# Another place for the feed-forward steps of the last two batches, and the last addition and store in two halves

## The chip, the cores and the metric

The kernel runs on one core of one Trainium2 chip. The metric is the device time of one execution in microseconds; 862.51 us is the median of three runs of the kernel before.

## What is computed

The reference is one decoder layer on x of 8 batches x 128 rows x 512 columns, float32: a latent attention with 128 heads, a cross attention with 32 query heads and 8 key heads, and a feed-forward with a router. Each is added to x after a layer norm. Only the third part is touched by the change:

```python
gate_logits = jnp.einsum('bsd,ed->bse', x, gate_w)
weights, selected = jax.lax.top_k(gate_logits, K)            # E = 8, K = 2
weights = jax.nn.softmax(weights.astype(jnp.float32), axis=2).astype(x.dtype)
result = jnp.einsum('bsd,od->bso', x, base_w) + base_b
w_full = jnp.sum(jax.nn.one_hot(selected, E, dtype=x.dtype) * weights[..., None], axis=2)
low = jnp.einsum('bsd,erd->ebsr', x, lora_A)                 # R = 16
lora_out = jnp.einsum('ebsr,eor,bse->bso', low, lora_B, w_full)
result = result + SCALING * lora_out
```

and the layer's output is `x + result`, where the x under the feed-forward is the normed one.

## The kernel before

The first 640 us are the latent attention, in 32 groups of four heads. Cross attention and feed-forward follow in one pipeline over all 8 batches, from about 640 us to the end. Every engine runs its own written-out list, a Python loop over u from FIRST = -8 to LAST - 1 = 40. A u below 32 is a unit of eight query heads, four units to a batch. With b, r = (u+1)//4, (u+1)%4 each step also does a piece of the batches on either side: r chooses the piece, b the batch. The order on an engine is the order of the code in this loop; engines wait for each other by semaphores, and each runs its list strictly in turn.

The steps after the last cross attention unit are the ones at issue. Batches are counted from 0 here, so the seventh is batch 6 and the eighth batch 7. For one batch v the feed-forward goes through these stages:

- x2 (L1104, VectorE): the cross attention's product is added to xs.
- norm_stats(2, v) (L1008 to L1010, VectorE) takes mean and variance; inverse(2, v) (L547, GpSimd) takes the power -0.5; norm_rows(2, v) (L1017, VectorE) writes the normed rows pn. GpSimd then adds the bias to xs (L555, semaphore s_xb).
- norm_turn(2, v) (L1432, TensorE) transposes pn into PSUM bank bF[0]; norm_high (L709, ScalarE) copies it as float16, Ah; norm_low (L1023, VectorE) keeps the remainder, Al.
- The gate product (L1156 through parts, 12 matmuls of 136 columns, agh and agl) writes the router's logits and the low-rank values into bank bF[1] = 7; ScalarE copies them to low (L753).
- gate_first (L1053 to L1061, VectorE) ranks the 8 logits, ScalarE takes the exponential (L745), gate_last (L1066 to L1071) makes the two weights and multiplies low by them.
- TensorE transposes low (L1444), ScalarE copies it as lowT (L742), and the low-rank product (L1462, float32) is added to the base product (base, L1156 with bwh and bwl, 12 matmuls of 512 columns) that waits in its own PSUM bank.
- x3 (L1088, VectorE) adds that bank to xs, and SyncE stores the batch (L434, result).

base_bank puts the base product of batches 0 to 5 into bank 7, that of batches 6 and 7 into banks 2 and 3. Bank 7 is also that of the gate product and of the cross attention's output product. Before each of these writes the helper take makes TensorE wait for whoever read the bank last:

```python
if r == 2:
    if 0 <= b - 2 < B:
        v = b - 2
        pe.wait_ge(n_tl[2], v + 1)
        take(bF[1], s_ge, v + 1)
```

So the gate product of batch 6 (u = 33) waits for x3 of batch 5, which reads bank 7 at u = 32. Behind that gate product, in the same step of TensorE's list, stand the four transposes of the last attention rows (L1477), which lead to O2h (L759), O2l (L1093) and the output product of batch 7. x_outputs (L1041 and L1045, VectorE) divides one unit's attention output by its sums and writes it to O2.

The last steps have these numbers: u = 32 is r = 1 with x3 of batch 5, norm_low and norm_turn of batch 6; u = 33 is r = 2; u = 34 is r = 3 with x2 of batch 7; u = 35 is r = 0 with norm_rows of batch 7; u = 36 is r = 1 with x3 and the low-rank product of batch 6 and the turn of batch 7; u = 37 is the gate product of batch 7; u = 40 has the low-rank product and x3 of batch 7.

Of the kernel before, what the change touches and what calls it, by code (L numbers as in the profile page):

```python
# [9 lines left out]
ALU = mybir.AluOpType  # L10
# [45 lines left out]
def build(nc, x, ctxT, pos, wdkr, wup, wqr, wo, xwq, xwkv, xwo, bw, ag, lb, bb, out):  # L56
    es = ExitStack()
    with es:
# [207 lines left out]
        def base_bank(v):  # L266

            return bF[1] if v < B - 2 else 2 + v % 2
# [48 lines left out]
        def _(sp):  # L317
# [114 lines left out]
            def result(b):  # L432
                sp.wait_ge(s_x3, b + 1)
                sp.dma_start(out[b], xs[:, b, :]).then_inc(s_out, 16)  # L434
# [7 lines left out]
            sp.wait_ge(s_out, 16 * B)  # L442
# [145 lines left out]
        def _(act):  # L588
# [145 lines left out]
            for u in range(FIRST, LAST):  # L734
                b, r = (u + 1) // KT, (u + 1) % KT
                turned_out(u)
                if r == 1 and 0 <= b - 3 < B:
                    v = b - 3
                    act.wait_ge(s_lt, v + 1)
                    if v >= 2:  # L740
                        act.wait_ge(s_f, v - 1)
                    nc.scalar.activation(lowT[:, v % 2], PS[:, 0, 3 * S:], ACT.Copy, scale=WS).then_inc(s_lT, 1)  # L742
# [3 lines left out]
                if r == 1:  # L746
                    norm_high(2, b - 2, bF[0], s_f)
# [25 lines left out]
        def _(dve):  # L773
# [275 lines left out]

            def gate_first(b):  # L1050
# [29 lines left out]
            for u in range(FIRST, LAST):  # L1080
                b, r = (u + 1) // KT, (u + 1) % KT
                if r == 1:
                    norm_low(2, b - 2, bF[0])
                    if 0 <= b - 3 < B:
                        v = b - 3
                        dve.wait_ge(s_f, v + 1)
                        dve.wait_ge(s_xb, v + 1)
                        nc.vector.scalar_tensor_tensor(xs[:, v, :], PS[:, base_bank(v), :], 1 / WS, xs[:, v, :],  # L1088
                                                       ALU.mult, ALU.add).then_inc(s_x3, 1)
# [17 lines left out]
                if 0 <= u - 1 < NU:  # L1107
                    x_outputs(u - 1)
                if r == 0:
                    norm_rows(2, b - 2)  # L1110
                    if 0 <= b + 1 < B:
# [13 lines left out]
                if r == 3:  # L1125
                    if b - 1 == B - 1:
                        norm_stats(2, b - 1)
                    if 0 <= b - 2 < B:
                        gate_last(b - 2)
                    if b - 1 < B - 1:  # L1130
                        norm_stats(2, b - 1)
# [18 lines left out]
        def _(pe):  # L1150
# [284 lines left out]
            for u in range(FIRST, LAST):  # L1435
                b, r = (u + 1) // KT, (u + 1) % KT
                if u == -2:
                    pe.wait_ge(s_x1, B)
                if r == 1 and 0 <= b - 3 < B:
# [15 lines left out]
                if r == 1:  # L1455
# [7 lines left out]
                    norm_turn(2, b - 2, bF[0])  # L1463
# [73 lines left out]
```

## Time and profile before

| what | value |
|---|---|
| median of three runs | 862.51 us (861.93 to 864.9) |
| the profiled execution, its own time | 860.44 us |
| its span in the profile | 858.5 us |
| mean granted TensorE clock | 0.98 |
| busy share of TensorE, VectorE, ScalarE, GpSimd | 93%, 75%, 66%, 68% |

A time in the profile is counted from the span's start. The span is that of the instructions; the execution's own time is 1.9 us longer. Rows give start, duration, engine, line and operation; in brackets stands how long the engine sat idle before it and for whom. PE is TensorE, PEld its weight load, DVE VectorE, ACT ScalarE, POOL GpSimd, SPq the queue of SyncE.

### The profile page before, as it was taken

To read this page: it belongs to the slowest core of one execution; us is meant where nothing else is said; L and a number is where in the kernel's file an instruction comes from. 1 tells how busy PE (TensorE), PEld (TensorE's weight loads), DVE (VectorE), ACT (ScalarE), POOL (GpSimd) and SP (SyncE) were. 2 spreads that over 40 slices of the span, in tenths; PEclk is the share of its full clock that TensorE was granted. 3 is DMA by queue.
4 is the path that set the end of the run, shared out by engine and by line. 5 is a ranking of instruction groups with operands and counts; after the bars stand their busy time and mean duration, and the time that the engine had idled before them with its cause. 6 is when DMAs were issued, how large, how long until landed. Compare 5 with 4: busy or idle time off the path is not lost.

```text
span 858.5 us, 17869 instructions
## 1 busy us (share of the span) xinstructions
PE 796.8 (93%) x5624; PEld 393.2 (46%) x5624; DVE 641.3 (75%) x1209; ACT 568.0 (66%) x1045; POOL 583.0 (68%) x493
## 2 busy tenths in 40 slices
PE   4999999999999999999999999999838688999986
PEld 3464444445444444444454444444313344555442
DVE  7867676767677888767888767788687567888754
ACT  4757777777777778777777777777530455555541
POOL 7747888888788888888788878885443323333210
PEclk9999999999999999999999999999978789999999
DMA  9345355434334343445323443432130000000001
GB/s 337 111 166 147 87 161 173 133 93 107 109 90 106 83 111 79 101 102 125 90 78 95 107 109 93 109 90 59 29 89 0 1 2 2 15 13 15 13 13 38
DMA packets 51227, 74.69 MB, mean 87 GB/s; under 512 B 9968, under 2 KB 33520, under 8 KB 50672
## 3 DMA queue, kind: packets, MB, share of 16 engines
q1 hardware_dynamic: 51184, 74.18, 31.7%
q8 instruction: 20, 0.33, 0.2%
q14 instruction: 23, 0.19, 0.1%
HBM read 38.16 MB, written 18.87 MB: 66 GB/s over the span
## 4 chain that ended last, share of the span: by engine, by line
PE 83%; DVE 9%; ACT 2%; issue 2%; SPq 1%; DMA 1%; POOL 0%; DVEq 0%; ACTq 0%
PE PS L1204 39%; PE PS L1156 8%; PE PS L1240 7%; PE PS L1272 6%; PE PS L1274 6%; PE PS L1289 5%; PE PS L1417 2%; PE PS L1424 1%; PE PS L1250 1%; PE PS L1386 1%; PE PS L1403 1%; PE PS L1432 1%; PE PS L1331 1%; PE PS L1462 1%; DVE xm L1031 1%
## 5 line engine op out<-in xcount | busy, mean ns | idle before, releaser
L496 POOL TENSOR_TENSOR Pl<-PR,Ph 128x512 f16<-128x512 f32 x254 | 285.8, 1157 | 24.4 <-ACT Ph L672 24.4
L665 ACT ACTIVATE PR<-PS 128x512 f32<-128x512 f32 x256 | 152.7, 597 | 130.8 <-PE PS L1274 124.4
L799 DVE TENSOR_REDUCE mneg<-PS 128x4 f16<-128x512 f32 x256 | 172.1, 685 | 36.8 <-PE PS L1240 34.6
L1204 PE MATMUL PS<-XTh,Wh 128*128 128x512 f16 x512 | 194.6, 380 | 0.0
L1204 PE MATMUL PS<-XTh,Wl 128*128 128x512 f16 x512 | 193.7, 378 | 0.0
L1204 PE MATMUL PS<-XTl,Wh 128*128 128x512 f16 x512 | 193.4, 378 | 0.0
L787 DVE SCALAR_TENSOR_TENSOR QS<-PS,QC 64x512 f16<-64x512 f32 x256 | 175.4, 685 | 19.7 <-ACT QC L597 15.7
L597 ACT ACTIVATE QC<-PS 64x512 f16<-64x512 f32 x256 | 150.9, 589 | 10.6 <-PE PS L1204 4.3
L672 ACT ACTIVATE Ph<-PR 128x512 f16<-128x512 f32 x256 | 139.3, 617 | 0.0
L1240 PEld LDWEIGHTS PS<-KC,QC 112*128 112x128 f16 x1024 | 78.8, 97 | 62.0 <-issue 2.5
L478 POOL TENSOR_TENSOR Wh<-Wraw,wscale 128x1024 f16<-128x1024 f32 x32 | 60.6, 1893 | 67.1 <-PE PS L1204 63.9
L1240 PE MATMUL PS<-KC,QC 112*128 112x128 f16 x1024 | 99.3, 219 | 0.0
L1272 PE MATMUL PS<-QC,KC 113*128 113x512 f16 x256 | 97.7, 382 | 0.0
L1274 PE MATMUL PS<-QS,KS 128*128 128x512 f16 x256 | 97.2, 379 | 0.0
L1204 PEld LDWEIGHTS PS<-XTh,Wh 128*128 128x128 f16 x512 | 49.9, 97 | 65.0 <-issue 25.9
L547 POOL TENSOR_TENSOR rstd<-rstd,power 128x1 f32<-128x1 f32 x16 | 8.8, 550 | 103.2 <-DVE rstd L1010 103.2
L1204 PEld LDWEIGHTS PS<-XTh,Wl 128*128 128x128 f16 x512 | 49.4, 97 | 61.2
L892 DVE TENSOR_SCALAR mT<-PS 16x128 f16<-16x128 f16 x64 | 13.6, 212 | 79.3 <-PE PS L1250 79.3
L484 POOL TENSOR_TENSOR Wl<-Wraw,Wh 128x1024 f16<-128x1024 f32 x32 | 68.2, 2132 | 2.5
L1204 PEld LDWEIGHTS PS<-XTl,Wh 128*128 128x128 f16 x512 | 49.7, 97 | 38.9
L482 POOL TENSOR_TENSOR Wraw<-Wraw,wscale 128x1024 f32<-128x1024 f32 x32 | 60.6, 1895 | 0.2
L1331 PE MATMUL PS<-wo_sb,U 128*128 128x512 f32 x64 | 34.9, 680 | 13.0 <-DVE U L966 11.6
(214 smaller groups left out, 1165.6 us busy)
## 6 DMA issues: line engine op xcount, KB each, us to landing
Wraw<-in_wqr SPq DMA_DIRECT2D x32, 512.0 KB, 5.1
QS<-QC SPq DMA_DIRECT2D x64, 256.0 KB, 3.2
head_outputs<-OS SPq DMA_DIRECT2D x256, 40.0 KB
q_content_parts<-stg SPq DMA_DIRECT2D x12, 256.0 KB, 2.9
k_content_parts<-stg SPq DMA_DIRECT2D x12, 256.0 KB, 3.1
QC<-q_content_parts SPq DMA_DIRECT2D x128, 24.0 KB
KC<-k_content_parts SPq DMA_DIRECT2D x32, 96.0 KB
xs<-in_x SPq DMA_DIRECT2D x8, 256.0 KB, 4.3
```

What stands on the lines that cost most here:

```text
L484: nc.gpsimd.tensor_tensor(Wl[:, par], Wraw[:, par], Wh[:, par], ALU.subtract).then_inc(s_ws, 1)
L496: nc.gpsimd.tensor_tensor(Pl[:, b], PR[:, b % 4], Ph[:, b], ALU.subtract).then_inc(s_pl, 1)
L597: nc.scalar.activation(QC[0:RD, par, t, 2 * p + h, :], PS[RD * h:RD * (h + 1), bQ[c % 2], :], ACT.Copy, scale=1 / WS).then_inc(s_qh, 1)
L665: nc.scalar.activation(PR[:, b % 4, :], PS[:, bB[b % 2], :], ACT.Exp, scale=ATT_SCALE).then_inc(s_e, 1)
L672: nc.scalar.activation(Ph[:, b, :], PR[:, b % 4, :], ACT.Copy).then_inc(s_ph, 1)
L787: nc.vector.scalar_tensor_tensor(QS[0:RD, par, t, j, :], PS[RD * h:RD * (h + 1), bQ[c % 2], :], 1 / WS, QC[0:RD, par, t, j, :], ALU.mult, ...
L799: nc.vector.tensor_reduce(mneg[:, par, b // 4, :, b % 4], PS[:, bA[b % 2], :].rearrange("p (j k) -> p j k", j=GH), AX.X, ALU.max, negate=T ...
L1156: last = mm(PS[:, bank, 0:c1 - c0], xt[:, k], wt[:, k, c0:c1], start=(start and k == 0 and n == 0), stop=(stop and k == KT - 1 and n == 2))
L1204: last = mm(PS[:, bQ[c % 2], :], wt[:, par, k, p * P:(p + 1) * P], xt[:, k, sl], start=(k == 0 and n == 0), stop=(k == KT - 1 and n == 2))
L1240: last = mm(PS[:, bA[b % 2], j * S:(j + 1) * S], QC[0:MROW, par, b // 4, j, b % 4 * S:(b % 4 + 1) * S], KC[0:MROW, par, b * S:(b + 1) * S] ...
L1272: mm(PS[:, bB[b % 2], :].rearrange("p (j q) -> p j q", j=GH), KC[0:MROW + 1, par, b * S:(b + 1) * S], QC[0:MROW + 1, par, t, :, b % 4 * S: ...
L1274: mm(PS[:, bB[b % 2], :].rearrange("p (j q) -> p j q", j=GH), KS[:, b * S:(b + 1) * S], QS[:, par, t, :, b % 4 * S:(b % 4 + 1) * S], start ...
```

## The change

Line numbers in the headings of the hunks are those of the files.

- VectorE, u = 32: x3 of batch 5 stands behind x_outputs of unit 31 and no longer ahead of it.
- VectorE, u = 35: gate_last of batch 6 stands behind norm_rows of batch 7 (it was ahead of it, in u = 34).
- TensorE, u = 36: norm_turn of batch 7 stands ahead of the transpose of low and the low-rank product of batch 6; ScalarE's norm_high of batch 7 stands ahead of its copy of lowT.
- x3 of batch 7 becomes two additions of 256 columns, and its store two transfers of 128 rows x 256 columns; the last wait counts 9 stores.
- In x3 the wait for the bias (s_xb) stands ahead of that for the low-rank product (s_f), for all batches.

```diff
@@ -430,8 +430,10 @@
                     sp.dma_start(KQ[row:row + 1, u % 4, 0:UQ, :], xmT[REP * h:REP * (h + 1), u % 2, :]).then_inc(s_xmd[u % 2], 16)
 
             def result(b):
-                sp.wait_ge(s_x3, b + 1)
-                sp.dma_start(out[b], xs[:, b, :]).then_inc(s_out, 16)
+                for i in range(2 if b == B - 1 else 1):
+                    c = slice(i * DM // 2, (i + 1) * DM // 2) if b == B - 1 else slice(0, DM)
+                    sp.wait_ge(s_x3, b + 1 + i)
+                    sp.dma_start(out[b][:, c], xs[:, b, c]).then_inc(s_out, 16)
 
             for u in range(NU):
                 x_maxima(u)
@@ -439,7 +441,7 @@
                     result(u // KT - 3)
             for b in range(B - 3, B):
                 result(b)
-            sp.wait_ge(s_out, 16 * B)
+            sp.wait_ge(s_out, 16 * (B + 1))
 
         @block.gpsimd
         def _(pool):
@@ -734,6 +736,8 @@
             for u in range(FIRST, LAST):
                 b, r = (u + 1) // KT, (u + 1) % KT
                 turned_out(u)
+                if r == 1 and b - 2 == B - 1:
+                    norm_high(2, b - 2, bF[0], s_f)
                 if r == 1 and 0 <= b - 3 < B:
                     v = b - 3
                     act.wait_ge(s_lt, v + 1)
@@ -743,7 +747,7 @@
                 if r == 3 and 0 <= b - 2 < B:
                     act.wait_ge(s_gx, b - 1)
                     nc.scalar.activation(ex[:], ex[:], ACT.Exp).then_inc(s_gy, 1)
-                if r == 1:
+                if r == 1 and b - 2 != B - 1:
                     norm_high(2, b - 2, bF[0], s_f)
                 if r == 2 and 0 <= b - 2 < B:
                     v = b - 2
@@ -1047,6 +1051,14 @@
                 last.then_inc(s_xon, 1)
                 dve.wait_ge(s_xon, u + 1)
 
+            def x3(v):
+                dve.wait_ge(s_xb, v + 1)
+                dve.wait_ge(s_f, v + 1)
+                for i in range(2 if v == B - 1 else 1):
+                    c = slice(i * DM // 2, (i + 1) * DM // 2) if v == B - 1 else slice(0, DM)
+                    nc.vector.scalar_tensor_tensor(xs[:, v, c], PS[:, base_bank(v), c], 1 / WS, xs[:, v, c], ALU.mult, ALU.add
+                                                   ).then_inc(s_x3, 1)
+
             def gate_first(b):
                 dve.wait_ge(s_ge, b + 1)
                 lg = low[:, b % 2, E * R:AG]
@@ -1081,12 +1093,8 @@
                 b, r = (u + 1) // KT, (u + 1) % KT
                 if r == 1:
                     norm_low(2, b - 2, bF[0])
-                    if 0 <= b - 3 < B:
-                        v = b - 3
-                        dve.wait_ge(s_f, v + 1)
-                        dve.wait_ge(s_xb, v + 1)
-                        nc.vector.scalar_tensor_tensor(xs[:, v, :], PS[:, base_bank(v), :], 1 / WS, xs[:, v, :],
-                                                       ALU.mult, ALU.add).then_inc(s_x3, 1)
+                    if 0 <= b - 3 < B and b - 3 != B - 3:
+                        x3(b - 3)
                 if r == 2 and 0 <= b - 1 < B:
                     v = b - 1
                     dve.wait_ge(s_oT, v + 1)
@@ -1106,8 +1114,12 @@
                         dve.wait_ge(s_x2, v + 1)
                 if 0 <= u - 1 < NU:
                     x_outputs(u - 1)
+                if r == 1 and b - 3 == B - 3:
+                    x3(b - 3)
                 if r == 0:
                     norm_rows(2, b - 2)
+                    if b - 2 == B - 1:
+                        gate_last(B - 2)
                     if 0 <= b + 1 < B:
                         v = b + 1
                         dve.wait_ge(s_xq, v + 1)
@@ -1125,7 +1137,7 @@
                 if r == 3:
                     if b - 1 == B - 1:
                         norm_stats(2, b - 1)
-                    if 0 <= b - 2 < B:
+                    if 0 <= b - 2 < B and b - 2 != B - 2:
                         gate_last(b - 2)
                     if b - 1 < B - 1:
                         norm_stats(2, b - 1)
@@ -1436,6 +1448,8 @@
                 b, r = (u + 1) // KT, (u + 1) % KT
                 if u == -2:
                     pe.wait_ge(s_x1, B)
+                if r == 1 and b - 2 == B - 1:
+                    norm_turn(2, b - 2, bF[0])
                 if r == 1 and 0 <= b - 3 < B:
                     v = b - 3
                     pe.wait_ge(s_lw, v + 1)
@@ -1460,7 +1474,8 @@
                             base(v)
                         pe.wait_ge(s_lT, v + 1)
                         mm(PS[:, base_bank(v), :], lowT[:, v % 2], lb_sb[:], start=False, stop=True).then_inc(s_f, 1)
-                    norm_turn(2, b - 2, bF[0])
+                    if b - 2 != B - 1:
+                        norm_turn(2, b - 2, bF[0])
                 if r == 2:
                     if 0 <= b - 2 < B:
                         v = b - 2
```

VectorE's list from Al of batch 6 (u = 32) to O2l of batch 7 (u = 33), before:

```order
L1023 TENSOR_TENSOR Al<-PS,Ah 128x512 [waits normed_high2]
L1088 SCALAR_TENSOR_TENSOR xs<-PS,xs 128x512 [waits bias_added,ffn_ready]
L1041 RECIPROCAL rz<-PS 128x2x2x2 [waits xo_turned]
L1045 TENSOR_TENSOR O_135<-PS,rz 128x2x32 [waits dve_chain]
L1045 TENSOR_TENSOR O_135<-PS,rz 128x2x32
L1093 TENSOR_TENSOR O2l<-PS,O2h 128x512 [waits oT_high,xo_out]
```

and in the changed kernel:

```order
L1027 TENSOR_TENSOR Al<-PS,Ah 128x512 [waits normed_high2]
L1045 RECIPROCAL rz<-PS 128x2x2x2 [waits xo_turned]
L1049 TENSOR_TENSOR O_135<-PS,rz 128x2x32 [waits dve_chain]
L1049 TENSOR_TENSOR O_135<-PS,rz 128x2x32
L1059 SCALAR_TENSOR_TENSOR xs<-PS,xs 128x512 [waits ffn_ready,bias_added,xo_out]
L1101 TENSOR_TENSOR O2l<-PS,O2h 128x512 [waits oT_high]
```

The addition of batch 5 moved past the three instructions of x_outputs.

VectorE's list from the variance of batch 7 (u = 34) to x3 of batch 6 (u = 36), before:

```order
L1010 TENSOR_SCALAR rstd<-mv 128x1 [waits dve_chain]
L1066 SCALAR_TENSOR_TENSOR ex<-rank,ex 128x8 [waits gate_exp]
L1067 TENSOR_REDUCE mx<-ex 128x1 [waits dve_chain]
L1068 RECIPROCAL mx<-mx 128x1 [waits dve_chain]
L1069 TENSOR_SCALAR ex<-ex,mx 128x8 [waits dve_chain]
L1071 TENSOR_TENSOR low<-low,ex 128x128 [waits dve_chain]
L1017 TENSOR_SCALAR pn<-xs,mv,rstd 128x512 [waits normed_turned2,rstd_ready2,low_weighted]
L1023 TENSOR_TENSOR Al<-PS,Ah 128x512 [waits normed_high2]
L1088 SCALAR_TENSOR_TENSOR xs<-PS,xs 128x512 [waits bias_added,ffn_ready]
```

and in the changed kernel:

```order
L1014 TENSOR_SCALAR rstd<-mv 128x1 [waits dve_chain]
L1021 TENSOR_SCALAR pn<-xs,mv,rstd 128x512 [waits normed_turned2,rstd_ready2]
L1078 SCALAR_TENSOR_TENSOR ex<-rank,ex 128x8 [waits gate_exp]
L1079 TENSOR_REDUCE mx<-ex 128x1 [waits dve_chain]
L1080 RECIPROCAL mx<-mx 128x1 [waits dve_chain]
L1081 TENSOR_SCALAR ex<-ex,mx 128x8 [waits dve_chain]
L1083 TENSOR_TENSOR low<-low,ex 128x128 [waits dve_chain]
L1027 TENSOR_TENSOR Al<-PS,Ah 128x512 [waits normed_high2,low_weighted]
L1059 SCALAR_TENSOR_TENSOR xs<-PS,xs 128x512 [waits ffn_ready,bias_added]
```

The normed rows of batch 7 moved ahead of the five instructions of gate_last of batch 6.

TensorE's list at u = 36, from the last matmul of the base product of batch 6 to the first of the gate product of batch 7, before:

```order
L1156 MATMUL PS<-bwh,Al 128x512
L1444 MATMUL PS<-ident,low 128x128 [waits xmax_out,kq_out,low_weighted]
L1462 MATMUL PS<-lb_sb,lowT 128x512 [waits lowT_out]
L1432 MATMUL PS<-ident,pn 128x128 [waits oT_low,normed2]
L1432 MATMUL PS<-ident,pn 128x128 x3
L1156 MATMUL PS<-agh,Ah 128x136 [waits x2_ready,normed_low2]
```

and in the changed kernel:

```order
L1168 MATMUL PS<-bwh,Al 128x512
L1444 MATMUL PS<-ident,pn 128x128 [waits oT_low,normed2]
L1444 MATMUL PS<-ident,pn 128x128 x3
L1458 MATMUL PS<-ident,low 128x128 [waits xmax_out,kq_out,low_weighted]
L1476 MATMUL PS<-lb_sb,lowT 128x512 [waits lowT_out]
L1168 MATMUL PS<-agh,Ah 128x136 [waits x2_ready,normed_low2]
```

The four transposes of pn moved ahead of the two steps on low and lowT; the gate product stands behind both in either list.

## Rows read from the trace of the kernel before

**Rows 1.** The page's part 4, the chain that ended last by engine.
```profile
PE 83%; DVE 9%; ACT 2%; issue 2%; SPq 1%; DMA 1%; POOL 0%; DVEq 0%; ACTq 0%
```
**Rows 2.** The chain in order of time, 835 to 843 us: start us, us, what.
```profile
836.10 0.69 DVE xs L1088
...
836.93 0.87 PE PS L1156 x12
...
838.27 0.61 ACT O2h L759
...
838.93 0.40 issue
839.33 0.70 DVE O2l L1093
```
**Rows 3.** Timeline of TensorE and VectorE, 827 to 837 us.
```profile
827.84 0.44 PE L1424 MATMUL PS<-ident,OW 128*128 128x128 f32 x2 [0.50 <-ACT OW L769]
...
828.39 0.21 DVE L1041 RECIPROCAL rz<-PS 128x8 f32<-128x8 f32 x1 [1.29 <-PE PS L1424]
...
835.90 0.44 PE L1424 MATMUL PS<-ident,OW 128*128 128x128 f32 x2 [0.50 <-ACT OW L769]
...
836.70 0.20 DVE L1041 RECIPROCAL rz<-PS 128x8 f32<-128x8 f32 x1
836.93 0.35 DVE L1045 TENSOR_TENSOR O<-PS,rz 128x64 f32<-128x64 f32 x2
```
**Rows 4.** The chain in order of time, 844 to 856 us.
```profile
845.53 0.30 DVE low L1071
...
846.58 1.13 PE PS L1462 x2
...
848.78 0.02 issue
848.81 0.70 DVE Al L1023
...
849.56 0.90 PE PS L1156 x12
850.48 0.29 ACT low L753
...
855.41 0.69 DVE xs L1088
```
**Rows 5.** Timeline of VectorE, TensorE and GpSimd around the third layer norm's steps.
```profile
844.85 0.55 POOL L547 TENSOR_TENSOR rstd<-rstd,power 128x1 f32<-128x1 f32 x1 [10.93 <-DVE rstd L1010]
...
847.54 0.60 PE L1432 MATMUL PS<-ident,pn 128*128 128x128 f32 x4
...
753.62 0.55 DVE L1017 TENSOR_SCALAR pn<-xs,mv,rstd 128x512 f32<-128x512 f32 x1
...
754.68 0.41 DVE L794 TENSOR_TENSOR rt<-PS,sinq 128x256 f32<-128x256 f32 x1
755.01 0.41 DVE L795 TENSOR_TENSOR rt<-PS,sinq 128x256 f32<-128x256 f32 x1
```
**Rows 6.** DMA: the stores (L434), the last one's packets, two small transfers' packets (822 to 826 us).
```profile
L434 SPq DMA_DIRECT2D y<-xs x8: 332/438/439, 747.7 to 856.1; - x8
DMA to landing us min/median/max: 2.0/2.1/2.4
q1 hardware_dynamic: 144, 0.26, 27.8%
q1 hardware_dynamic: 16, 0.00, 0.3%
```
**Rows 7.** Instruction transfers: the page, the window of 838.5 to 839 us, VectorE's stop at 688 us.
```profile
q8 instruction: 20, 0.33, 0.2%
q8 instruction: 1, 0.02, 11.6%
690.81 1.29 DVE L1031 TENSOR_REDUCE xm<-PS 128x4 f16<-128x512 f32 x2 [2.51 <-issue]
```

## The prediction

> **What bounds the kernel now.** The page's chain by engine [rows 1] is the first view: 83% of the path that sets the end runs through TensorE. The change leaves everything before 836 us as it is, so of that path only the last 22 us count. There, beside small waits, no work of a second kind runs: the chain in order of time goes from one engine to the next, and whatever makes one of its links later or earlier moves the end by as much. I read it in two pieces, 835 to 843 us [rows 2] and 844 us to the end [rows 4], and looked into the timelines for what stands beside it [rows 3, 5]. The store at the end needs the DMA views [rows 6], and one gap of VectorE the instruction transfers [rows 7].
>
> In the first piece [rows 2] the reader is to see that x3 of batch 5 is itself a link: VectorE adds it at 836.10 for 0.69 us, and the gate product of batch 6, which has to wait for bank 7, starts at 836.93, 0.14 us behind its end. The transposes of the last attention rows stand behind that gate product on TensorE, and on them hang O2h, O2l and the output product of batch 7. In the second piece [rows 4] the low-rank product of batch 6 and then the turn of batch 7 come one after the other on TensorE, and from the gate product of batch 7 at 849.56 on there is one line of steps to the last addition at 855.41.
>
> **Part A, x3 of batch 5 behind x_outputs.** This costs. x_outputs waits for the transposes at 835.90, which end at 836.34; at 827.84 to 828.28 the same pair was followed by VectorE 0.11 us later [rows 3], so it can start at 836.45, 0.25 us before its start of 836.70. The last of its three instructions ends 837.28 - 836.70 = 0.58 us later, at 837.03 [rows 3]. x3 follows after some 0.03 us of semaphore (what Al of batch 7 took behind its copy, 848.78 to 848.81 [rows 4]) and takes 0.69: it ends at 837.75, and the gate product starts 0.14 us later, at 837.89 in place of 836.93: 0.96 us late. The output rows that were given the earlier place are ready at 837.03 instead of 837.28, but TensorE reaches their transposes only behind the gate product, so that gain has no taker.
>
> Not all of the 0.96 arrives. O2h ends at 838.88, yet O2l starts at 839.33, with 0.40 us marked as issue [rows 2] where Al needed 0.03 us. Near it lies a transfer of instructions in 838.5 to 839 us, and a stop of 2.51 us with nothing to wait for is seen at 688 us too [rows 7]. I read both as VectorE waiting for its next code. If that stop runs from about 837 us to 839.33, a later O2h hides it: O2h ends at 838.88 + 0.96 = 839.84, O2l starts at 839.87, 0.54 us later than before. The ends are +0.54 and +0.96 (the stop remains as long as it is); nothing in the rows makes a gain possible while the gate product waits for bank 7. I take **+0.54**, since a stop that begins before the wait is nearest to what the 688 us row shows.
>
> **Part B, rows and turn of batch 7 ahead of gate_last and low-rank product of batch 6.** Before, GpSimd's power is done at 844.85 + 0.55 = 845.40, but pn stands behind gate_last, which runs until low's end at 845.53 + 0.30 = 845.83 [rows 4, 5]. Now pn can start at 845.43 and, at 0.55 us [rows 5], end at 845.98. gate_last is about 1.1 us long (from the variance just ahead of the power's start to 845.83), so low is weighted at 847.1 in place of 845.83. TensorE turns pn at 846.02, for 0.60 us [rows 5]; a copy to float16 takes ScalarE 0.61 (O2h [rows 2], of the same shape), to 847.27, and the remainder Al takes VectorE about 0.70 (O2l [rows 2], same shape), to 848.0. The low-rank product used to start 846.58 - 845.83 = 0.75 us behind low [rows 4], with a transpose and a copy between; now it starts at 847.85. ScalarE is free of Ah at 847.27 and so doesn't hold it. TensorE's next work started 847.54 - 846.58 = 0.96 us after the product's start [rows 4, 5]. So the gate product of batch 7 starts at 848.81, while its Al has been ready since 848.0: what is late next is the low-rank product of batch 6, not the rows. The gain is 849.56 - 848.81 = **-0.75**. Its ends: -0.58 if the product holds the next matmul for its whole 1.13 us [rows 4], and -0.9 if low's path is 0.15 shorter than worked out.
>
> x3 of batch 6 on VectorE starts when that product ends, near 849.0, and is done at 849.7; gate_first of batch 7 needs low at 848.81 + 0.92 + 0.29 = 850.02, where 0.92 is 850.48 - 849.56 [rows 4]. So it stays covered by 0.3 us. The base product of batch 7 runs beside the gate's chain in both kernels and shifts with it. The 5.9 us from the gate product to the last addition (855.41 - 849.56) keep their order.
>
> **Part C, last addition and store by halves.** An addition of 256 columns takes 0.41 us and the next one starts 0.33 us behind it [rows 5] (two on PSUM of that shape). The first half is done 0.41 us and both are done 0.74 us after the start, in place of 0.69 [rows 4]. SyncE issues a store in 0.44 us [rows 6], so the second can be issued 0.41 + 0.44 = 0.85 us after the start, 0.16 later than the whole one was. What it has for that is less to move: the last whole store takes 144 packets and 27.8% of 16 engines over 2.5 us, 11.1 us of engine time, or 85 ns for each of its 128 large packets of 2 KB, and 16 tiny packets take 0.3% of 4 us x 16, 12 ns each [rows 6]. A packet of 1 KB lies between; an estimate in the middle is 48 ns, and 8 per engine save 0.29 us. Net **-0.13**; the ends are +0.40 (1 KB costs 85 ns, the second half queues behind the first) and -0.42 (12 ns).
>
> The Trainium skill, DMA: Bandwidth & Descriptors, section Anatomy of one DMA, gives some 2.0 us of fixed cost and bytes over 436 GB/s, and its rules ask to coalesce small transfers. By it the half saves 0.30 us of moving, for which the second issue pays 0.16, so the sum would be the same within 0.01. [...]
>
> **Part D, the order of two waits.** In x3 the bias was added long before the product ends, at each of the two places that count, so the product's wait covers it in either order: 0.
>
> **Sum.** +0.54 - 0.75 - 0.13 = -0.34 us. The profiled execution took 860.44 us, so the changed kernel's would be 860.10. The median of three is 2.07 us above the profiled one, so on its scale I expect 862.2. No change in the clock is counted: all this lies within about 22 us, with engines idle no longer at a stretch than now.
>
> **Rivals.**
> *The code boundary lands on x3 of batch 5 (slower).* VectorE's stop belongs to a place in its instruction list. Between Al and O2l the list keeps the same instructions, but O2l's neighbours change, and the waits are packed otherwise. If the first instruction on the new code is now x3 and no longer O2l, VectorE stops ahead of an addition that TensorE waits for. The stop lasted 839.33 - 837.28 = 2.05 us at O2l and 2.51 at 688 us [rows 2, 3, 7]. From 837.03 on, x3 starts between 839.08 and 839.54, the gate product at 839.91 to 840.37, 3.0 to 3.4 us late; the old stop of 0.42 at O2l is gone, so A is +2.6 to +3.0, and the sum +1.7 to +2.1: 864.2 to 864.6, say 864.4. For it: the boundary lies within two or three instructions of x3. Against: the instruction count ahead of O2l is nearly the same, and then the stop falls where it did. It decides from one instruction's shift on. Chance 0.15. The Trainium skill, Advanced Engine Details and Errata, section ISA Cache, has lines of 16 KB or 256 instructions and two lines in all. The page's 20 transfers with 0.33 MB, 16.5 KB each [rows 7], agree with it.
>
> *Nothing is hidden.* The stop at O2l stays (A +0.96) and a packet of 1 KB costs as much as one of 2 KB (C +0.40): +0.96 - 0.75 + 0.40 = +0.61, 863.1. The tiny packets' 12 ns in [rows 6] speaks against the second half of it. Chance 0.15.
>
> *A isn't paid.* If the gate product of batch 6 did not have to wait for x3, or the earlier rows helped someone, the sum would be B and C alone: -0.88, 861.6. The 0.14 us between x3 and the gate product [rows 2] speak against it. Chance 0.1.
>
> **How the numbers follow.** The forecast has a chance of 0.6, at 862.2. A measurement of this kernel tells about 0.3% from no change, 2.6 us; forecast, second and third rival lie within it by far, and the first by 0.5 us or more unless C and B come at their bad ends. That gives slower 0.06, faster 0.03 (nothing in 22 us of chain offers 2.6 us but a stop that goes elsewhere), same 0.91. The three runs of before lie from 0.6 below to 2.4 above their median, so the range takes the rivals' 861.6 and 864.4 and some of that: 860.8 to 864.6.
>
> **What would show it.** Right: the gate product of batch 6 starts near 837.9 behind x3; O2l near 839.9 with no issue gap ahead of it; pn of batch 7 before gate_last; low-rank product of batch 6 directly ahead of the gate product of batch 7, which starts near 849.56 + 0.54 - 0.75 = 849.35; two additions of some 0.41 us at the end, and a second store with a shorter landing. Wrong: a gap of 2 us on VectorE ahead of x3 of batch 5 (first rival), one left ahead of O2l (second), the gate product of batch 6 still near 836.9 (third), or Al of batch 7 as the last thing its gate product waits for.

## The result, and the profile after

The changed kernel took 866.16 us (median of 22 runs, 863.77 to 870.28), the kernel before 864.11 us (22 runs taken beside them, 861.37 to 866.07). The ratio is 1.0034 [1.0021, 1.0048]: slower by 0.34%, or 2.9 us [1.8, 4.1], where 862.2 us and no measurable change were forecast. (The ratio is not the quotient of the two medians, which lie 2.05 us apart.) The profiled execution of the changed kernel took 865.04 us, with a span of 863.2 us against 858.5.

The first look is at the whole. The page of the changed kernel: the granted clock in 40 slices, and the chain by engine, to be held against [rows 1].

```profile
PEclk9999999999999999999999999999969799999998
...
PE 83%; DVE 9%; ACT 2%; issue 2%; DMA 2%; SPq 1%; POOL 0%; DVEq 0%; ACTq 0%
```

Shares of a whole span don't show 4 us. The same stretches in windows do. The windows of the changed kernel, with the columns us, busy time (and instructions) of PE, PEld, DVE, ACT and POOL, then the granted clock, the DMA share and GB/s:

```profile
834.00:838.20 4.20, 2.20 (x16) 0.88 (x15) 1.95 (x5) 0.98 (x2) 0.29 (x1) 1.00 0.01 2
838.20:845.20 7.00, 5.57 (x24) 3.05 (x25) 1.92 (x8) 1.09 (x3) 0.00 (x0) 0.51 0.12 40
845.20:852.00 6.80, 4.79 (x23) 2.17 (x22) 4.52 (x11) 0.87 (x2) 1.82 (x2) 1.00 0.00 0
852.00:855.60 3.60, 3.60 (x16) 2.02 (x17) 0.78 (x2) 0.28 (x1) 0.00 (x0) 0.53 0.03 13
855.60:860.10 4.50, 3.81 (x14) 1.32 (x12) 2.25 (x12) 0.48 (x2) 0.00 (x0) 1.00 0.13 48
```

and two of the same stretches of the kernel before:

```profile
838.20:845.20 7.00, 5.16 (x25) 2.27 (x24) 4.00 (x15) 0.81 (x2) 0.35 (x1) 1.00 0.03 11
852.00:855.60 3.60, 2.48 (x8) 0.73 (x6) 1.43 (x8) 0.28 (x1) 0.00 (x0) 1.00 0.00 0
```

The column to read is the clock: in two stretches, of 7.0 and 3.6 us, TensorE was granted 0.51 and 0.53, that is its lower level of 1.2 GHz with a bit of the higher at the edge, where the kernel before had 2.4 GHz (1.00) in both.

The chain of the changed kernel in order of time answers to [rows 2] and [rows 4]:

```profile
837.37 0.70 DVE xs L1059
...
838.21 1.40 PE PS L1168 x12
839.61 0.87 PE PS L1492 x4
...
840.50 0.61 ACT O2h L763
...
841.13 0.70 DVE O2l L1101
...
841.88 4.40 PE PS L1168 x12
...
846.37 0.70 DVE xs L1112
...
849.91 0.88 DVE ex L1081
...
851.86 1.94 PE PS L1476 x2
853.80 1.37 PE PS L1168 x12
...
860.17 0.42 DVE xs L1059
```

The gate product of batch 6 takes 1.40 us instead of 0.87, the output product of batch 7 4.40 instead of 2.78, the low-rank product with two matmuls 1.94 instead of 1.13, the gate product of batch 7 1.37 instead of 0.90. All are the same instructions as before. The gap ahead of O2l is 0.02 us instead of 0.40.

The timeline of the changed kernel shows what stood ahead of each stretch, and one more thing. The number in brackets is the engine's idle time ahead of the row:

```profile
838.21 0.22 PE L1168 MATMUL PS<-agh,Ah 128*128 128x136 f16 x1 [1.51 <-DVE xs L1059]
...
849.47 0.66 PE L1444 MATMUL PS<-ident,pn 128*128 128x128 f32 x4 [0.61 <-DVE pn L1021]
849.49 1.27 POOL L557 TENSOR_TENSOR xs<-xs,bias 128x512 f32<-128x512 f32 x1 [0.66 <-DVE pn L1021]
849.91 0.87 DVE L1081 TENSOR_SCALAR ex<-ex,mx 128x8 f32<-128x8 f32 x1
...
851.16 0.33 PE L1458 MATMUL PS<-ident,low 128*128 128x128 f32 x1 [1.04 <-DVE low L1083]
```

TensorE stood idle for 1.51 us ahead of the gate product of batch 6, where [rows 2, 3] leave 0.59 (the transposes end at 836.34, the gate product starts at 836.93). Behind it the clock is low. Before the second stretch it stood idle for 0.61 and, but for four transposes, again for 1.04 us. That second gap is so long because gate_last's scaling (L1081) of 128 x 8 values took 0.87 us. It now runs beside GpSimd's addition of the bias, and both end within 0.02 us of each other: 849.49 + 1.27 = 850.76 and 849.91 + 0.87 = 850.78. The same step took 0.23 us before, and the addition began only behind it, since the normed rows pn stood behind gate_last. The timeline of the kernel before:

```profile
845.27 0.23 DVE L1069 TENSOR_SCALAR ex<-ex,mx 128x8 f32<-128x8 f32 x1
...
845.86 0.55 DVE L1017 TENSOR_SCALAR pn<-xs,mv,rstd 128x512 f32<-128x512 f32 x1
...
846.49 1.27 POOL L555 TENSOR_TENSOR xs<-xs,bias 128x512 f32<-128x512 f32 x1 [1.09 <-DVE pn L1017]
```

So that starts that differ between executions don't enter, all kernels are compared by their **tail**: from the start of ScalarE's copy Ah of batch 6 (834.86 us before, 835.23 after) to the end of the span. It is 23.64 us before and 27.97 after, +4.33. From link to link of the chain it divides like this:

| piece | before | after | difference | of what |
|---|---|---|---|---|
| Ah of batch 6 to its gate product | 2.07 | 2.98 | +0.91 | x3 waits for x_outputs |
| gate product and transposes, to O2h | 1.34 | 2.29 | +0.95 | half clock |
| O2h to O2l | 1.06 | 0.63 | -0.43 | stop gone |
| O2l to x2 of batch 7 | 3.61 | 5.24 | +1.63 | half clock |
| x2 to the gate product of batch 7 (849.56, 853.60) | 6.62 | 7.23 | +0.61 | new order -0.81, scaling +0.64, half clock +0.78 |
| gate product of batch 7 to the last addition | 5.85 | 6.57 | +0.72 | half clock |
| last addition to the end | 3.09 | 3.03 | -0.06 | halves |

In the fifth row the half clock is 1.74 us in place of 0.96 from the low-rank product's start to the next matmul, the scaling 0.87 in place of 0.23, and the -0.81 is what remains. The half clock adds up to +4.1 us, the waits to +0.48, the rest to -0.2.

### The profile page after: what moved, and what is told of

Read it like the earlier page. It is cut to its first block, busy times and chain, and to the rows that moved or that the text cites. A ratio compares the mean times of both kernels' runs of the same rounds, so it can differ in the third digit from the quotient of the medians.

```text
span 863.2 us, 17871 instructions
## 1 busy us (share of the span) xinstructions
PE 801.1 (93%) x5624; PEld 395.2 (46%) x5624; DVE 642.4 (74%) x1210; ACT 568.0 (66%) x1045; POOL 583.5 (68%) x493
## 4 chain that ended last, share of the span: by engine, by line
PE 83%; DVE 9%; ACT 2%; issue 2%; DMA 2%; SPq 1%; POOL 0%; DVEq 0%; ACTq 0%
PE PS L1216 39%; PE PS L1168 8%; PE PS L1252 7%; PE PS L1284 6%; PE PS L1286 6%; PE PS L1301 5%; PE PS L1429 2%; PE PS L1436 1%; PE PS L1262 1%; PE PS L1398 1%; PE PS L1415 1%; PE PS L1476 1%; PE PS L1444 1%; PE PS L1343 1%; DVE xm L1035 1%
## 5 line engine op out<-in xcount | busy, mean ns | idle before, releaser
L711 ACT ACTIVATE Ah<-PS 128x512 f16<-128x512 f32 x16 | 9.5, 597 | 59.9 <-PE PS L1444 59.9
```

## The experiments

**The theory.** The idle time of TensorE is the cause, not the waits themselves: where it stands idle longer in this thin tail, its clock is halved behind. Two places do so: part A's 1.51 us, and part B's gap of 1.04 us, which comes of the collision at L1081. **The rivals:** the halves or the turned waits cost more than counted; half clock in this stretch is an accident of one execution that has no tie to the change; the new order itself is at fault through its waits. Where a kernel is said to have fillers, these are extra matmuls into a bank that nobody reads any more; fill(6) is six of them.

### Each part alone

e1_x3_only is the kernel before with x3 of batch 5 behind x_outputs:

```diff
-                    if 0 <= b - 3 < B:
+                    if 0 <= b - 3 < B and b - 3 != B - 3:
...
                     x_outputs(u - 1)
+                if r == 1 and b - 3 == B - 3:
+                    v = b - 3
...
```

> The kernel before with x3 of batch 5 moved behind x_outputs of unit 31, and nothing else. Theory of the clock: TensorE then stands idle for some 1.5 us ahead of the gate product of batch 6, the granted clock falls to 0.5 near 838.5 us, the gate product takes some 1.4 us and the output product of batch 7 some 4.4 us, and the kernel is slower than before by 2.5 to 4 us (0.54 of waiting, the rest clock). Rival, waiting alone: the granted clock stays at 1.0 and the kernel is 0.5 to 1.0 us slower, and the loss of the changed kernel comes from its other parts.

e2_without_x3_move is the changed kernel with x3 of batch 5 back in its old place:

```diff
-                    if 0 <= b - 3 < B and b - 3 != B - 3:
+                    if 0 <= b - 3 < B:
                         x3(b - 3)
...
-                if r == 1 and b - 3 == B - 3:
-                    x3(b - 3)
```

> The changed kernel with x3 of batch 5 back ahead of x_outputs; everything else of the change stays. Theory of the clock: the idle ahead of the gate product of batch 6 is 0.6 us as before, the granted clock stays at 1.0 to the end of the gate product, and the kernel is 0.1 to 0.9 us faster than before and 3 to 4 us faster than the changed one. Rival, part B loses by its own gap: the clock falls only in the second place, near 852 us, and the kernel is 0.5 to 2 us slower than before.

e3_rows_only is the kernel before with the hunks on norm_high, norm_turn and gate_last alone:

```diff
                     norm_rows(2, b - 2)
+                    if b - 2 == B - 1:
+                        gate_last(B - 2)
...
+                if r == 1 and b - 2 == B - 1:
+                    norm_turn(2, b - 2, bF[0])
                 if r == 1 and 0 <= b - 3 < B:
```

> The kernel before with the rows and the turn of batch 7 ahead of gate_last and the low-rank product of batch 6, and nothing else. The step's worth was put at -0.75 us. If the scaling of the router's weights (the tensor_scalar in gate_last) now stands beside GpSimd's bias addition and takes 0.87 us there in place of 0.23, the gain is about -0.1 us. If in addition the clock falls behind the wait for low, near 848 to 850 us, it is 0.5 to 2 us slower.

e4_halves_only is the kernel before with the last addition and store in halves:

```diff
+                        for i in range(2 if v == B - 1 else 1):
+                            c = slice(i * DM // 2, (i + 1) * DM // 2) if v == B - 1 else slice(0, DM)
...
-            sp.wait_ge(s_out, 16 * B)
+            sp.wait_ge(s_out, 16 * (B + 1))
```

> The kernel before with the last addition and store in two halves, and nothing else. Predicted -0.13 us, between -0.42 and +0.40; nothing else in the trace differs, the granted clock is 1.0 to the end of the last product.

| kernel | tail us | against before | half clock behind the 1st, 2nd place | ratio [interval] |
|---|---|---|---|---|
| before | 23.64 | | no, no | |
| changed | 27.97 | +4.33 | yes, yes | 1.0034 [1.0021, 1.0048] |
| e1_x3_only | 26.74 | +3.10 | yes, no | 1.0047 [1.0029, 1.0064] |
| e2_without_x3_move | 25.07 | +1.43 | no, yes | 1.0011 [0.9995, 1.0028] |
| e3_rows_only | 25.11 | +1.47 | no, yes | 1.0020 [1.0003, 1.0037] |
| e4_halves_only | 23.58 | -0.06 | no, no | 1.0015 [0.9998, 1.0031] |

Windows of e1_x3_only:

```profile
836.00:839.00 3.00, 0.99 (x11) 0.30 (x6) 1.95 (x5) 0.94 (x2) 0.00 (x0) 1.00 0.00 0
839.00:846.00 7.00, 5.58 (x25) 2.99 (x26) 1.92 (x8) 1.09 (x3) 0.00 (x0) 0.51 0.11 41
846.00:860.00 14.00, 10.41 (x51) 4.62 (x49) 7.24 (x25) 1.64 (x5) 1.82 (x2) 1.00 0.05 19
```

and of e3_rows_only:

```profile
836.00:850.00 14.00, 9.48 (x60) 4.65 (x58) 7.50 (x23) 2.67 (x6) 2.06 (x3) 1.00 0.06 20
850.00:854.00 4.00, 3.58 (x16) 2.17 (x17) 1.38 (x3) 0.28 (x1) 0.00 (x0) 0.58 0.00 0
```

One move of one addition brings the first stretch, the order of rows and gate_last the second, and each without the other. The two parts alone make +3.10 + 1.47 = +4.57, near the whole's +4.33. For e2 I had held the gain of part B likelier; it came out as the other case named there, and e3 as the last of its three cases. The scaling took 0.87 us in e2 and e3. The halves move the tail by -0.06, and e4's ratio, whose interval takes in 1, is no evidence of a cost. The turned waits have no kernel of their own, but e2 is rows, halves and turned waits together, and 1.43 - 1.47 + 0.06 leaves 0.02 us for them. That rival falls. e1 and e4 came as the theory expected.

### The idle time filled, the waits left

In e5_fill_first_gap TensorE, before it waits for bank 7, does six matmuls of 512 columns into a bank that is free (0.22 us each). All else is the changed kernel:

```diff
+            def fill(n):
+                for i in range(n):
+                    mm(PS[:, 4, :], bwh[:, 0, 0:P], bwl[:, 0, :], start=True, stop=True)
...
                         pe.wait_ge(n_tl[2], v + 1)
+                        if v == B - 2:
+                            fill(6)
                         take(bF[1], s_ge, v + 1)
```

> The changed kernel with six extra float16 matmuls of 512 columns into PSUM bank 4, which nobody reads then, ahead of the gate product of batch 6: TensorE is busy for about 1.3 of the 1.5 us that it stands idle there. The product keeps its time and its wait for x3. Theory of the clock: the granted clock stays at 1.0 through the output product of batch 7, which takes 2.8 us in place of 4.4, and the part from the copy Ah of batch 6 to the end shrinks by some 2.4 us, from 27.97 to about 25.5 us; the second fall near 852 us may stay. Rival: the clock falls for another cause than TensorE's idle time (load of another engine, power), then it falls here too and nothing is gained.

e6_bias_late is the changed kernel with GpSimd's last bias addition behind gate_last of batch 6:

```diff
                     pool.wait_ge(n_xn[2], v + 1)
+                    if v == B - 1:
+                        pool.wait_ge(s_lw, B - 1)
                     nc.gpsimd.tensor_tensor(xs[:, v, :], xs[:, v, :], bias[:], ALU.add).then_inc(s_xb, 1)
```

> The changed kernel with GpSimd's bias addition of batch 7 made to wait until gate_last of batch 6 is done. Theory of the collision: the scaling in gate_last takes 0.23 us in place of 0.87, low is weighted 0.64 us earlier, and the part from Ah of batch 6 to the end shrinks by 0.3 to 1.0 us. Rival: the 0.87 us has another cause (code, semaphores) and stays with GpSimd idle beside it.

As expected within 0.5 us, e5's tail was 25.05 us, 2.92 shorter than the changed kernel's by six more matmuls (ratio to before 1.0006 [0.9986, 1.0025]). The first stretch stayed at 1.00, the second fell as before, 0.57 in 851 to 855 us. e6's tail was 25.85 (1.0019 [1.0000, 1.0038]), 2.12 shorter where I had expected 0.3 to 1.0. The timeline of e6_bias_late says why:

```profile
849.72 0.23 DVE L1083 TENSOR_SCALAR ex<-ex,mx 128x8 f32<-128x8 f32 x1
...
850.33 0.33 PE L1460 MATMUL PS<-ident,low 128*128 128x128 f32 x1 [0.40 <-DVE low L1085]
850.42 1.26 POOL L559 TENSOR_TENSOR xs<-xs,bias 128x512 f32<-128x512 f32 x1 [1.78 <-DVE low L1085]
```

The scaling is back at 0.23 us, so it had waited for the bias addition. TensorE's gap ahead of the transpose of low shrank with it from 1.04 to 0.40 us, and the second fall did not come. From x2 to the gate product of batch 7 e6 takes 851.99 - 846.19 = 5.80 us, against 6.62 before. That is part B at full clock and without the collision: -0.82. No kernel fills this second gap and leaves the collision in: in e6, and in e8, e10 and e11 further on, the addition on GpSimd is moved too. So for the second place the runs show that the longer gap and the addition inside it go together with the fall, and that it is the length of the gap is argued from the first place.

### A cause taken away rather than filled

The wait of the gate product for x3 exists because the base product of batch 5 lies in bank 7. In e7_base5_own_bank it lies in bank 3:

```diff
-            return bF[1] if v < B - 2 else 2 + v % 2
+            return bF[1] if v < B - 3 else 2 + v % 2
...
                         if v < B - 2:
-                            take(bF[1], s_x3, v + 1)
+                            if v < B - 3:
+                                take(bF[1], s_x3, v + 1)
                             base(v)
```

> The changed kernel with the base product of batch 5 in bank 3, so that the gate product of batch 6 no longer waits for x3 of batch 5. It starts near 0.1 us behind the transposes of OW; the output rows' transposes start some 1.4 us earlier than in the changed kernel. Theory: the idle ahead of it is gone, the clock stays at 1.0 there, and the part from Ah of batch 6 to the end is 3 to 4.5 us shorter than the changed kernel's 27.97. Rival: the idle moves behind it (TensorE waits for O2l up to 2.5 us) and the clock falls there, so that 1.5 us or more of the loss stays.

e8_fill_all is e6 with fill(6) ahead of the gate product of batch 6, fill(5) ahead of the output product of batch 7 and fill(4) behind the turn of batch 7:

```diff
                     norm_turn(2, b - 2, bF[0])
+                    fill(4)
...
+                        if v == B - 2:
+                            fill(6)
                         take(bF[1], s_ge, v + 1)
...
+                        if v == B - 1:
+                            fill(5)
                         pe.wait_ge(s_oTl, v + 1)
```

> The changed kernel with the late bias addition and extra matmuls into bank 4 in three gaps: six ahead of the gate product of batch 6, five ahead of the output product of batch 7, four behind the turn of batch 7. Theory: the granted clock is 1.0 to the last product, the two parts of the change are then worth what was worked out for waits alone (+0.54 and -0.75), and from Ah of batch 6 to the end it takes 23.3 us, the time of the kernel before (23.64) or 0.3 less. Rival: over 25 us, then more than clock and collision is lost.

e7's tail was 23.46 us, 4.51 shorter than the changed kernel's, where 3 to 4.5 were expected, and its ratio 0.9985 [0.9966, 1.0003] (one run of 3037 us left out). With the gate product right behind the transposes there is no first gap, and no first fall. The second gap is 1.04 us as before, and the clock is 0.57 in 850 to 854 us. e8's tail was 23.51 (0.9996 [0.9977, 1.0015]), 0.2 above the 23.3 that was expected and that the prediction's sum comes to. The window of e8_fill_all over the whole tail:

```profile
836.00:858.90 22.90, 17.09 (x94) 8.06 (x91) 11.53 (x39) 3.20 (x10) 1.81 (x2) 1.00 0.10 35
```

### The parts of the prediction at full clock, and the better kernel

e9_x3_filled is e1 with fill(6) and fill(5) in the two places ahead of the gate product and the output product; e10_rows_filled is e3 with e6's wait and fill(2), fill(6) and fill(4) in the three places:

```diff
                         pe.wait_ge(n_tl[2], v + 1)
+                        if v == B - 2:
+                            fill(6)
...
                         v = b - 1
+                        if v == B - 1:
+                            fill(5)
```

> The kernel before with x3 of batch 5 behind x_outputs, as in e1, and extra matmuls into bank 4 in two gaps (six ahead of the gate product of batch 6, five ahead of the output product of batch 7), so that the clock is held. It sizes the wait alone. From the copy Ah of batch 6 to the end: 23.64 us in the kernel before, 26.74 in e1. Theory: the part costs 0.54 us of waiting and the rest of e1's 3.10 is clock, so 24.1 to 24.3 us here. Rival: the stop ahead of O2l stays (+0.96), 24.6 us.

> The kernel before with rows and turn of batch 7 ahead, as in e3, the bias addition of batch 7 behind gate_last, and extra matmuls into bank 4 in three gaps (two, six and four). It sizes the order alone. Theory: -0.75 us against the kernel before's 23.64, so 22.8 to 23.0 us from Ah of batch 6 to the end. Rival: the order is worth nothing even at full clock and without the collision, 23.5 us or more.

e12_bank_bias has the edits of e7 and e6 together; e11_bank_bias_fill adds fill(5) and fill(4) to it:

```diff
-            return bF[1] if v < B - 2 else 2 + v % 2
+            return bF[1] if v < B - 3 else 2 + v % 2
...
+                    if v == B - 1:
+                        pool.wait_ge(s_lw, B - 1)
```

> e11 without any extra matmul. It tells whether the clock falls behind the turn of batch 7 also when low comes 0.64 us earlier. Theory: the idle between the turn and the transpose of low shrinks from 1.04 to 0.4 us, as in e6, where the clock didn't fall in that place; then 21.5 to 22.3 us as e11. Rival: it falls, 22.8 us or more.

> The changed kernel with the base product of batch 5 in bank 3, the bias addition of batch 7 behind gate_last, and extra matmuls ahead of the output product of batch 7 (five) and behind its turn (four). e7 took 23.46 us from Ah of batch 6 to the end with a fall of the clock and the collision in it. Theory: without both 21.5 to 22.3 us, some 1.5 us or 0.2% under the kernel before. Rival: the fillers stand in the way of the product they precede or the clock falls all the same, 23 us or more.

| kernel | tail us | against before | ratio [interval] |
|---|---|---|---|
| e9_x3_filled | 24.15 | +0.51 | 1.0017 [1.0004, 1.0031] |
| e10_rows_filled | 23.01 | -0.63 | 0.9990 [0.9975, 1.0005] |
| e11_bank_bias_fill | 22.11 | -1.53 | 0.9986 [0.9969, 1.0003] |
| e12_bank_bias | 21.87 | -1.77 | 0.9977 [0.9963, 0.9991] |

e1 and e9 differ by eleven matmuls that compute nothing of use, and e9's tail is 2.59 us shorter. Its window of 839 to 862 us has the clock at 1.00. What is left of part A at full clock is +0.51. In e8 and e10 the filler costs a little itself: the transpose of low starts 0.35 us behind low (in e8 848.43 against 847.79 + 0.29) where e6 needed 0.05. That is why e10 gives -0.63 and not -0.8. e9, e11 and e12 came out within what was expected, e10 0.01 us above it.

Windows of e12_bank_bias:

```profile
838.00:844.00 6.00, 4.58 (x32) 2.59 (x33) 3.43 (x13) 1.09 (x3) 0.00 (x0) 1.00 0.13 48
844.00:850.00 6.00, 4.62 (x22) 2.07 (x21) 3.88 (x11) 0.87 (x2) 1.81 (x2) 1.00 0.00 0
850.00:856.00 6.00, 4.77 (x28) 2.08 (x25) 3.29 (x14) 0.77 (x3) 0.00 (x0) 1.00 0.11 44
```

Without a filler the clock stays up: the first gap is gone and the second is 0.41 us. e11's fillers, with nothing left to hold, cost 0.24 us. e12's median is 860.40 us (12 runs) against 862.83 of the kernel before (35 runs beside it); by the ratio it is faster by 0.23%, 2.0 us [0.8, 3.2]. That is the lowest ratio and the shortest tail here, though several other intervals overlap its own.

Over all twelve and the two kernels at hand the profiles agree. The first fall is in the three (changed, e1, e6) that have the gap of 1.5 us unfilled, and in no other. The second is in the five (changed, e2, e3, e5, e7) in which the scaling is held up and TensorE idles 1.04 us ahead of the transpose of low with no filler, and in no other. An accident of one execution does not sort itself so. Of the executions without a profile only times and mean clocks are on record. In twelve of the thirteen kernels the tail's difference from before lies within the interval of the ratio, and in the changed kernel 0.2 us above it. The intervals are some 3 us wide, so they don't contradict the tails but can't confirm each of them.

## Why the prediction was wrong

**The step that failed** is one sentence at the end of the sum: "No change in the clock is counted: all this lies within about 22 us, with engines idle no longer at a stretch than now." It puts the clock at nothing, and its reason does not carry. Over the whole tail that reason is even true: TensorE's longest gap was 1.84 us before, and the changed kernel has none above 1.51. At the place that the change touches it is untrue by the prediction's own numbers. Part A moves the gate product from 836.93 to 837.89 while TensorE's work ahead of it still ends at 836.34, so its gap grows from 0.59 to 1.55 us (measured: 1.51). Behind that gap came 2.6 us of half clock, behind the second place 1.5 more, against a forecast sum of -0.34. The second term that the sum lacks is the collision of the scaling with the bias addition, 0.64 us (part B below).

**The clock.** Rows first: 0.51 behind a gap of 1.51 us, 1.00 behind the same gap with six matmuls in it. The Trainium skill, TensorE: Matmul & The Clock Gate, section Part 1: The HAM clock gate, puts it as "the default state is throttled, and activity releases the throttle"; the trace agrees in that the tails have only the levels 0.50 and 1.00 clear of an edge, and the lower one when TensorE has no work: 0.50 in 856 to 858 us of e4_halves_only, whose last product ends at 855.06. By that rule an edit that leaves TensorE idle longer between short bursts needs a case for the lower level in its forecast. Rows give its size: gate product +0.53, transposes +0.41, output product +1.62, 2.6 us for the first place.

**Part A, waits.** Forecast +0.54, measured +0.91 - 0.43 = +0.48 in the changed kernel, +0.51 in e9. The first term, +0.96 of waiting for x3, was right in mechanism and size. The second, -0.42 for the stop ahead of O2l, was right in size by luck. The gate product started 0.14 us behind x3, as forecast.

**The stop ahead of O2l.** It went, as forecast, but not for the reason given. The prediction took it as a stop of 2 us fixed to a place in VectorE's code that a later O2h hides. The chain of e2_without_x3_move, where x3 is not moved, has it again:

```profile
841.08 0.02 DVEq L1100
841.10 0.40 issue
841.50 0.70 DVE O2l L1101
```

and the timeline of VectorE in e7_base5_own_bank has none:

```profile
839.28 0.69 DVE L1059 SCALAR_TENSOR_TENSOR xs<-PS,xs 128x512 f32<-128x512 f32 x1
840.63 0.69 DVE L1101 TENSOR_TENSOR O2l<-PS,O2h 128x512 f16<-128x512 f32 x1 [0.65 <-ACT O2h L763]
```

In e7 VectorE is busy with x3 until 839.97 and starts O2l 0.03 us behind O2h, so no stop of 2 us has room there. The stop of 0.40 us is in before, e2, e3, e4 and e10, where O2l follows x_outputs and the wait for O2h stands as an instruction of the queue ahead of it; it is in none of the kernels where x3 stands between, which carries the wait for x_outputs away from O2l. What makes it 0.40 us long is open. It was not tested by itself.

**Part B.** The order's gain was right: forecast -0.75, measured -0.81 in the changed kernel and -0.82 in e6. What the prediction missed is that pn also starts the bias addition on GpSimd. Before, pn stood behind gate_last, so the two did not run together. Now gate_last runs in the very time of that addition, and its scaling takes 0.64 us longer; in e6, e8, e10, e11 and e12, where the addition comes later, it takes 0.23 us again. The Trainium skill, SBUF — State Buffer, section SBUF: two separate sides, says that VectorE and GpSimd share one pair of ports, which one instruction holds to its end while the other waits, if VectorE's runs in a two-port mode or has two inputs in SBUF. The scaling that ends 0.02 us behind the addition agrees with it, if it runs in such a mode, which no run shows; the reduction and the reciprocal just ahead of it (0.17 us each) ran beside the addition without harm. By the prediction's own times TensorE would have stood idle for some 0.5 us between the turn (to 846.62) and low (847.1), and e6 has 0.40. The collision made it 1.04 us, and with that came the second fall: 0.78 + 0.72 = 1.5 us.

**Part C.** Forecast -0.13, measured -0.06 in the changed kernel and in e4. The middle value for a packet of 1 KB holds. DMA of the changed kernel, the two half stores over 859.8 to 863.2 us:

```profile
q1 hardware_dynamic: 288, 0.26, 23.1%
issues: line engine op xcount, KB each, median us to landing
y<-xs SPq DMA_DIRECT2D x2, 128.0 KB, 1.8
```

16 engines x 3.4 us x 23.1% = 12.6 us, less 32 tiny packets at 12 ns, over 256 packets is 48 ns each. From issue to landing the last store took 1.8 us in place of 2.0, so 0.2 and not 0.29 us came of it. The Trainium skill, DMA: Bandwidth & Descriptors, section Anatomy of one DMA, on which the prediction draws here, describes transfers that GpSimd issues. This store is SyncE's, so that its sum came near the forecast says nothing for either.

**The rivals.** The code boundary on x3 of batch 5 did not come: x3 started at 837.37, 0.02 us behind x_outputs. The kernel was slower, but by another cause, and by more: on the prediction's scale the result is 862.51 x 1.0034 = 865.4 us, above the rival's 864.4 and above the range's 864.6. "Nothing is hidden" and "A isn't paid" are refuted by the O2l row and by the gate product's start.

**What stays open.** The changed kernel's 22 runs lie in two groups, 863.8 to 866.4 (12) and 867.9 to 870.3 (10), and its profiled tail (+4.33) is just above the interval of the ratio (1.8 to 4.1 us). The mean granted clock on record is 0.970 to 0.975 in the first group and 0.968 to 0.970 in the second. By estimate, 0.004 less over 863 us is some 7 us more at the lower level, which costs up to 3.5 us where TensorE is busy; the second group is 3.9 us slower in the mean (869.0 against 865.1). The profiled execution is of the first group. Where in the kernel the clock fell in the second, one profile per kernel does not tell.

## What to carry to other kernels

In a tail where one engine hands to the next, read the gap that an edit opens on TensorE as well as the wait it adds: here 0.9 us more of idle time cost 0.5 us as a wait and 2.6 us as half clock on the matmuls behind it. Where a gap can't be closed, a few matmuls into a free bank can keep the clock, as in e5 and e9; closing it (another bank, so that the wait isn't there) gave more here, 21.87 us of tail in e12 against 23.51 with all gaps filled in e8. When steps on VectorE are put in another order, look also at what their semaphores start on GpSimd, and whether it now runs beside a short step on the path.

## What the hardware showed that was not expected

- The length of one gap does not decide alone. TensorE idled 1.84 us ahead of the output product at 840.07 and 1.42 us ahead of the gate product at 849.56 in the kernel before (rows below), and the clock stayed at 1.00. In the changed kernel the 1.51 us came behind a gap of 0.50 us and only 0.44 us of work (the transposes at 836.27), the 1.04 us behind a gap of 0.61 and 0.66 us of work. What the runs show is that these two places fall and that filling or closing them keeps the clock, not a length from which a gap costs.

```profile
840.07 0.39 PE L1156 MATMUL PS<-woh,O2h 128*128 128x512 f16 x1 [1.84 <-DVE O2l L1093]
...
849.56 0.23 PE L1156 MATMUL PS<-agh,Ah 128*128 128x136 f16 x1 [1.42 <-DVE Al L1023]
```

- A scaling of 128 x 8 values went from 0.23 to 0.87 us beside a GpSimd addition of 1.27 us, and back to 0.23 when the addition came later.
- The same code ahead of the tail reached Ah of batch 6 anywhere from 834.62 us (e4) to 839.39 us (e11) in the profiled executions. The granted clock in 640 to 660 us lay between 0.60 and 0.74, with 0.72 in e4 and 0.63 in e11, but 0.60 in e7, which came to Ah at 837.14, so that stretch alone does not set it. That scatter is larger than any edit here, which is why the tail was compared and not the span.
